# The running sum opens with the skip term, and a third buffer holds products of h and C

## What is computed

```python
dA = jnp.exp(dt[:, :, None] * A[None])
dBu = dt[:, :, None] * B[:, None, :] * u[:, :, None]

def step(hst, inp):
    dAt, dBut, Ct = inp
    hst = dAt * hst + dBut
    return (hst, hst @ Ct)
_, ys = lax.scan(step, jnp.zeros((D_INNER, D_STATE), h.dtype), (dA, dBu, C))
y = ys + u * D_skip
y = y * jax.nn.silu(z)
return y @ w_out
```

## Time and profile before

| | |
|---|---|
| median of 3 runs | 1579.28 us (1578.86 to 1580.91) |
| profiled execution | 1580.11 us |
| its span | 1578.3 us |
| TensorE busy | 1504.4 us, 95% |
| VectorE busy | 1360.7 us, 86% |
| GpSimd busy | 1134.1 us, 72% |
| ScalarE busy | 1025.7 us, 65% |
| TensorE's granted clock, mean | 0.986 |

### The profile page before, as it was taken

The page is one execution under the profiler, slowest core; times in us unless marked ns, Lnnn a source line. Parts: engine busy times, 40 slices in busy tenths (PEclk is TensorE's granted clock), DMA queues, the critical chain, the costliest instruction groups (busy, mean ns, idle before and its releaser), DMA issues. The chain is left out here.

```text
span 1578.3 us, 17939 instructions
## 1 busy us (share of the span) xinstructions
PE 1504.4 (95%) x4976; PEld 768.4 (49%) x4976; DVE 1360.7 (86%) x1617; ACT 1025.7 (65%) x2180; POOL 1134.1 (72%) x542
## 2 busy tenths in 40 slices
PE   7999999999999999999999999999997789999995
PEld 3444434444444444444444444444442235999994
DVE  7405999999999999999999999999999897667998
ACT  3254757666666767676767585757666755777774
POOL 0325989898989898989898898989898883000223
PEclk9999999999999999999999999999998899999998
DMA  9877767777777777676767777777752523000002
GB/s 364 336 244 275 256 230 243 246 252 243 257 244 259 244 238 263 233 260 240 244 238 259 243 249 254 248 252 248 252 190 73 181 74 118 16 0 1 0 0 107
DMA packets 65404, 322.46 MB, mean 204 GB/s; under 512 B 7036, under 2 KB 7088, under 8 KB 32437
## 3 DMA queue, kind: packets, MB, share of 16 engines
q1 hardware_dynamic: 54433, 302.21, 55.0%
q10 hardware_dynamic: 10900, 19.44, 4.2%
HBM read 309.27 MB, written 12.35 MB: 204 GB/s over the span
## 5 line engine op out<-in xcount | busy, mean ns | idle before, releaser
L655 PE MATMUL bank<-ring,xh 128*128 128x512 f32 x2048 | 956.7, 594 | 10.9 <-DVE xh L1296 8.1
L1428 DVE TENSOR_TENSOR_SCAN work<-bank,hstate,work 128x512 f32<-128x512 f32 x512 | 628.8, 1272 | 20.3 <-ACT bank L965 13.0
L655 PEld LDWEIGHTS bank<-ring,xh 128*128 128x128 f32 x2048 | 387.6, 190 | 462.6 <-issue 422.5
L1159 POOL TENSOR_TENSOR work<-work 128x1024 f32<-128x1024 f32 x210 | 495.8, 2361 | 85.5 <-DVE work L1369 77.1
L965 ACT ACTIVATE bank<-work,a_neg 128x512 f32<-128x512 f32 x512 | 344.6, 686 | 250.5 <-DVE work L1428 247.1
L1361 DVE TENSOR_TENSOR work<-work,bank 128x1024 f32<-128x1024 f32 x253 | 307.1, 1219 | 62.2 <-POOL work L1135 54.4
L1369 DVE TENSOR_TENSOR work<-work,bank 128x1024 f32<-128x1024 f32 x168 | 201.8, 1201 | 23.3 <-POOL work L1159 23.3
L541 PE MATMUL bank<-bc_parts,sel 96*128 96x512 bf16 x422 | 161.8, 384 | 23.5 <-DVE work L1361 22.6
L1245 POOL TENSOR_TENSOR work<-work 128x256 f32 x32 | 27.3, 854 | 213.2 <-ACT work L1032 213.2
L536 PE MATMUL bank<-work,w_sb 128*128 128x512 f32 (+2 forms) x352 | 175.3, 594 | 1.3 <-issue 0.8
L1104 POOL TENSOR_TENSOR work<-work 128x1024 f32<-128x1024 f32 x48 | 113.7, 2369 | 18.5 <-ACT work L839 18.4
(11 more groups left out here) (163 smaller groups left out, 1589.7 us busy)
## 6 DMA issues: line engine op xcount, KB each, us to landing
ring<-adj_t SPq DMA_DIRECT2D x256, 1024.0 KB, 5.4
xh<-c_scratch SPq DMA_DIRECT2D x34, 256.0 KB, 3.3
work<-c_scratch ACTq DMA_DIRECT2D x28, 256.0 KB, 5.9
c_two<-c_scratch ACTq DMA_DIRECT2D x28, 256.0 KB, 5.0
xh<-x_rows SPq DMA_DIRECT2D x16, 256.0 KB, 7.2
work<-x_t SPq DMA_DIRECT2D x16, 256.0 KB, 5.3
x_scratch<-work ACTq DMA_DIRECT2D x16, 256.0 KB, 3.6
work<-x_scratch SPq DMA_DIRECT2D x1, 4096.0 KB, 14.6
```

What stands on the lines that cost most here:

```text
L655: last = nc.tensor.matmul(mixed[:, :], xn[:, j, :], a, start=(j == 0), stop=(j == BLK - 1))
L1159: nc.gpsimd.tensor_tensor(out=acc, in0=hc[0] if n == 1 else acc, in1=hc[n % 2], op=ALU.add).then_inc(y_added, 1)
L1428: nc.vector.tensor_tensor_scan(hb[s % 2][:, h, :], da[h], (dbu_late[POOL_DBU.index(s)] if on_pool else dbu[s % 2])[:, h, :], hstate[:, HV ...
```

## The change

The accumulator `acc` takes over the role of `yv`. ScalarE writes the skip term of the chunk being scanned into `acc`, in slot 3 of the same k, once the gate of the chunk before has read `acc` (`y_ready`). GpSimd's `add(0)`, placed in slot 2 of its program ahead of `add(1)`, waits for the skip term and adds product 0; sixteen additions, all of the form acc + hc. The closing additions L1142 and L1348 go, and the gate reads `acc`. The buffer of `yv` becomes a third buffer for products: product n goes to `hc[(16c + n) % 3]` and waits for addition (or sum) n-3. The skip terms of the last two chunks stay in k = 17, and `dbu_late` uses `u[0]` instead of `acc`.

```diff
-        hc = [halves(carve(W2)) for _ in range(2)]
+        hc = [halves(carve(W2)) for _ in range(3)]
...
-        yv = halves(carve(W2))
...
+        def hc_of(c, n):
+            return hc[(DS * c + n) % 3]
...
-        dbu_late = [dt[0], dtu[0], acc]
+        dbu_late = [dt[0], dtu[0], u[0]]
...
                 def state_sum(n, c):
...
-                        pe.wait_ge(y_skip, k - 2)
+                        pe.wait_ge(hc_done, hc_count(NC - 3, DS - 1, False))
+                        wait(pe, y_skip, c - (NC - 2))
...
                 def skip(values):
                     for h in range(HV):
-                        last = nc.scalar.activation(yv[:, h, :], values[:, h, :], ACT.Copy, scale=V("d_skip", h))
+                        last = nc.scalar.activation(acc[:, h, :], values[:, h, :], ACT.Copy, scale=V("d_skip", h))
                     last.then_inc(skip_ready, 1)
 
                 def post_part(s):
-                    if s == 0 and k < NC + 2:
+                    if s == 0 and k == NC + 1:
+                        act.wait_ge(y_ready, NC - 2)
                         skip(u[q])
...
+                    if scan and not drains(k) and s == 3:
+                        wait(act, y_ready, cs)
+                        skip(u[par])
                     if scan and not drains(k) and s in C_LOAD:
                         load_c(C_LOAD[s])
...
-                        pool.wait_ge(y_added, (DS - 1) * (k - 2))
-                        pool.wait_ge(skip_ready, k - 2)
-                        nc.gpsimd.tensor_tensor(out=yv, in0=yv, in1=acc, op=ALU.add).then_inc(y_skip, 1)
...
-                    nc.gpsimd.tensor_tensor(out=by_step(yp), in0=by_token(yv), in1=by_token(sz[q]), op=ALU.mult).then_inc(y_ready, 1)
+                    nc.gpsimd.tensor_tensor(out=by_step(yp), in0=by_token(acc), in1=by_token(sz[q]), op=ALU.mult).then_inc(y_ready, 1)
 
                 def add(n):
 
                     wait_hc(pool, cs, n)
-                    if n == 1:
-                        wait_hc(pool, cs, 0)
-                    if n > 1:
-                        pool.wait_ge(y_added, (DS - 1) * cs + (n - 1))
-                    nc.gpsimd.tensor_tensor(out=acc, in0=hc[0] if n == 1 else acc, in1=hc[n % 2],
-                                            op=ALU.add).then_inc(y_added, 1)
+                    if n == 0:
+                        pool.wait_ge(skip_ready, cs + 1)
+                    else:
+                        pool.wait_ge(y_added, DS * cs + n)
+                    nc.gpsimd.tensor_tensor(out=acc, in0=acc, in1=hc_of(cs, n), op=ALU.add).then_inc(y_added, 1)
...
                     if drains(k):
-                        if n < 2:
-                            pool.wait_ge(y_added, (DS - 1) * (NC - 2))
-                        wait(pool, y_summed, DS * (cs - (NC - 2)) + (n - 1))
-                    elif n >= 2:
-                        pool.wait_ge(y_added, (DS - 1) * cs + max(n - 2, 1))
+                        if n < 3:
+                            pool.wait_ge(y_added, DS * (NC - 2))
+                        wait(pool, y_summed, DS * (cs - (NC - 2)) + (n - 2))
                     else:
-                        wait(pool, y_added, (DS - 1) * cs + (n - 1))
...
+                        wait(pool, y_added, DS * cs + n - 2)
...
                     elif scan and s >= 2:
+                        if s == 2:
+                            add(0)
                         add(s - 1)
...
                 def finish_y():
...
-                    if k == NC:
-                        dve.wait_ge(y_added, (DS - 1) * (NC - 2))
-                        nc.vector.tensor_tensor(out=yv, in0=yv, in1=acc, op=ALU.add).then_inc(y_skip, 1)
...
-                    wait(dve, y_added, (DS - 1) * cs + (max(n - 2, 1) if n >= 2 else n - 1))
-                    nc.vector.tensor_tensor(out=hc[n % 2], in0=hb[n % 2], in1=both(c_bank[n % 2]),
+                    wait(dve, y_added, DS * cs + n - 2)
+                    nc.vector.tensor_tensor(out=hc_of(cs, n), in0=hb[n % 2], in1=both(c_bank[n % 2]),
                                             op=ALU.mult).then_inc(hc_done, 1)
```

More of the change, by code:

```diff
@@ L582, in last_sums @@
                                 wait_hc(pe, NC - 1, n)
-                            last = nc.tensor.matmul(y_bank[h][:, :], ident, hc[n % 2][:, h, :], start=False, stop=(n == DS - 1))
+                            last = nc.tensor.matmul(y_bank[h][:, :], ident, hc_of(NC - 1, n)[:, h, :], start=False, stop=(n == DS - 1))
                         last.then_inc(y_half_done, 1)
@@ L590, in state_sum @@
                         pe.wait_ge(ident_ready, 2)
-                        pe.wait_ge(y_skip, k - 2)
+                        pe.wait_ge(hc_done, hc_count(NC - 3, DS - 1, False))
+                        wait(pe, y_skip, c - (NC - 2))
                     wait_hc(pe, c, n)
                     for h in range(HV):
-                        last = nc.tensor.matmul(y_bank[h][:, :], ident, hc[n % 2][:, h, :], start=(n == 0),
+                        last = nc.tensor.matmul(y_bank[h][:, :], ident, hc_of(c, n)[:, h, :], start=(n == 0),
                                                 stop=(n == DS - 1))
@@ L669, in step @@
                             for h in range(HV):
-                                nc.tensor.matmul(y_bank[h][:, :], ident, yv[:, h, :], start=False, stop=False)
+                                nc.tensor.matmul(y_bank[h][:, :], ident, acc[:, h, :], start=False, stop=False)
                         if k == NC:
@@ L1122, in pre_part @@
                         elif scan:
-                            pool.wait_ge(y_added, (DS - 1) * cs + 11)
+                            pool.wait_ge(y_added, DS * cs + 12)
                         else:
@@ L1165, in make_dbu @@
                     pool.wait_ge(scan_done, HV * DS * (NC - 1))
+                    if i == 2:
+                        pool.wait_ge(skip_ready, NC - 1)
                     nc.gpsimd.tensor_tensor(out=dbu_late[i], in0=dtu[par], in1=b_late[i].unsqueeze(1).broadcast_to([P, HV, CH]),
@@ L1180, in make_hc @@
                     if drains(k):
-                        if n < 2:
-                            pool.wait_ge(y_added, (DS - 1) * (NC - 2))
-                        wait(pool, y_summed, DS * (cs - (NC - 2)) + (n - 1))
-                    elif n >= 2:
-                        pool.wait_ge(y_added, (DS - 1) * cs + max(n - 2, 1))
-                    else:
-                        wait(pool, y_added, (DS - 1) * cs + (n - 1))
-                    nc.gpsimd.tensor_tensor(out=hc[n % 2], in0=hb[n % 2], in1=c.unsqueeze(1).broadcast_to([P, HV, CH]),
+                        if n < 3:
+                            pool.wait_ge(y_added, DS * (NC - 2))
+                        wait(pool, y_summed, DS * (cs - (NC - 2)) + (n - 2))
+                    else:
+                        wait(pool, y_added, DS * cs + n - 2)
+                    nc.gpsimd.tensor_tensor(out=hc_of(cs, n), in0=hb[n % 2], in1=c.unsqueeze(1).broadcast_to([P, HV, CH]),
                                             op=ALU.mult).then_inc(pool_hc_done, 1)
@@ L1317, in side_part @@
                     if drains(k):
-                        if post and k < NC + 2 and slot == (1 if k == NC else 2):
+                        if k == NC + 1 and slot == 2:
                             finish_y()
@@ L1345, in finish_y @@
                     dve.wait_ge(skip_ready, k - 2)
-                    if k == NC:
-                        dve.wait_ge(y_added, (DS - 1) * (NC - 2))
-                        nc.vector.tensor_tensor(out=yv, in0=yv, in1=acc, op=ALU.add).then_inc(y_skip, 1)
-                    else:
-                        dve.wait_ge(y_summed, DS)
-                        for h in range(HV):
-                            last = nc.vector.tensor_tensor(out=yv[:, h, :], in0=yv[:, h, :], in1=y_bank[h][:, :], op=ALU.add)
-                        last.then_inc(y_skip, 1)
+                    dve.wait_ge(y_summed, DS)
+                    for h in range(HV):
+                        last = nc.vector.tensor_tensor(out=acc[:, h, :], in0=acc[:, h, :], in1=y_bank[h][:, :], op=ALU.add)
+                    last.then_inc(y_skip, 1)
                 def both(ap):
@@ L1375, in make_last_hc @@
                     dve.wait_ge(scan_done, HV * DS * cs + HV * (n + 1))
-                    dve.wait_ge(y_summed, DS * (cs - (NC - 2)) + (n - 1))
+                    dve.wait_ge(y_summed, DS * (cs - (NC - 2)) + (n - 2))
                     for h in range(HV):
-                        nc.vector.tensor_tensor(out=hc[n % 2][:, h, :], in0=hb[n % 2][:, h, :], in1=c_bank[0][:, :],
+                        nc.vector.tensor_tensor(out=hc_of(cs, n)[:, h, :], in0=hb[n % 2][:, h, :], in1=c_bank[0][:, :],
                                                 op=ALU.mult).then_inc(last_hc, 1)
```

5 lines of the change are left out of this document (4 added, 1 removed).

## The result

The changed kernel took 1564.4 us (median of 4 runs, 1563.57 to 1567.1). The kernel before took 1580.1 us in four runs (1578.86 to 1581.81). The ratio is 0.9897, 95% interval 0.9885 to 0.9909: 1.0% faster, 15.7 us. The profiled execution took 1564.17 us with a span of 1562.3, against 1580.11 and 1578.3 before.

What follows compares the result with a forecast made beforehand. The prediction took TensorE's own 74.4 us a chunk as the bound. It summed 11.4 us (steady part), 2.8 (start of k=16) and 2.0 (k=17) to 16.2, giving 1563.1 us, range 1560.5 to 1573.

Steps and rivals of the forecast that it cites:

- What bounds: Periodic part: TensorE sets the pace, with 74.4 us of its own work in a chunk of 75.25 us.
- The wait at the turn: At each chunk's turn, VectorE's product 15 no longer waits for GpSimd's addition 13; VectorE gains 1.66 us a turn.
- The new wait w: Once a chunk VectorE's scan 5 waits for GpSimd's product 3, behind the skip term and additions 0 to 2: 1.5 us.
- Slack: VectorE's lead over TensorE at L1326: 0.4 us left; TensorE waits for nothing while the new scan wait is under 1.9.
- k=3: TensorE's wait at the turn to this chunk falls from 2.33 us by 1.55 to 0.78.
- k=4 to k=15: TensorE's waits of about 0.82 us at each of twelve turns go, 9.9 us in all; period 74.4 us.
- Start of k=16: VectorE loses the closing addition and waits around it; GpSimd caps the gain at 2.8 us, bounds 1.8 and 3.2.
- k=17: Chunk 15: GpSimd's waits for TensorE's sums go, so VectorE gains its 2.0 us of waits for products; bounds 0 and 2.7.
- A: Rival: the opening chain bounds; scan 5's wait is 1.9 to 2.9 us, VectorE sets the period, up to 1.0 x 12 lost; chance 0.22.
- B: Rival: nothing reaches the end; scan 5's wait is 2.9 us or a little above, time within 3 us of before; chance 0.08.
- C: Rival: slower; one more GpSimd instruction or equal delay in the opening chain, scan 5 waits 3.8 us, 1586 us; chance 0.06.
- D: Rival: the third buffer pays nothing in k=16 and 17 because TensorE's granted clock falls; 1568 us; chance 0.09.

Runs made afterwards that it cites:

- third_buffer_alone: The kernel before with three buffers for products of h and C; the sum's old opening and closing addition stay: 1565.65 us, ratio 0.9905.
- skip_twice: The changed kernel with ScalarE's skip term written twice, one after the other, 1.35 us more in the opening chain: 1584.16 us, ratio 1.0022.
- skip_slot2: The changed kernel with ScalarE's skip term one slot earlier, in slot 2: 1563.39 us, ratio 0.9885; run once more, 1563.41 us.
- product3_first: The changed kernel with GpSimd making product 3 before addition 2, skip term left in slot 3: 1564.51 us, ratio 0.9894.
- after_again: The changed kernel once more, unedited, as the measure beside other runs: 1566.52 us, ratio 0.9915.

## Why the prediction held, step by step

- *What bounds.* TensorE's own work of 74.4 us a chunk was right: 74.38 to 74.59 in every kernel where it doesn't wait for VectorE, and of that 0.1 to 0.2 are waits for the adjacency ring.
- *The wait at the turn.* Right. It is gone, and `third_buffer_alone` shows that the third buffer does it.
- *The new wait w.* The mechanism and place were right, the size was off: 2.03 for 1.5. The chain from the end of scan 2 (593.87) to the start of scan 5 (605.88) is 12.01 us where the sum said 11.7. GpSimd's part of it and ScalarE's are these rows:

```profile
593.90 0.69 ACT L970 ACTIVATE bank<-work,a_neg 128x512 f32<-128x512 f32 x1 [0.48 <-DVE work L1433]
594.53 0.19 ACT L952 ACTIVATE hstate<-work 128x2 f32<-128x2 f32 x1
594.63 1.32 ACT L902 ACTIVATE work<-work,v_sb 128x512 f32<-128x512 f32 x2
...
596.09 7.35 POOL L1167 TENSOR_TENSOR work<-work 128x1024 f32<-128x1024 f32 x3 [2.93 <-ACT work L902]
603.39 2.35 POOL L1195 TENSOR_TENSOR work<-work,c_two 128x1024 f32<-128x1024 f32 x1
```

  Exponential, small copy, skip and handoff took the 2.2 that they were given. The three additions took 7.30, not 6.93: each needs the one before it, and I had taken their pitch from two instructions that don't depend on each other (2.31), though the row of three dependent ones stood beside it (7.45 from 658.55 to 666.00). VectorE's own work meanwhile was 10.0, not 10.2. These two make the 0.5.
- *Slack.* The 0.4 forecast at L1326 came out as 0.45, with w larger than forecast by 0.5. VectorE is a little quicker elsewhere (its scans 1267 ns in the mean for 1272, its waits for the exponential 0.3 us a chunk for 0.5), which covers some 0.4 of it; the rest I haven't traced. The threshold of 1.9 was near the true one and stood in the wrong place: `skip_twice` shows that TensorE meets the delay at ScalarE's copies and silu, from w about 2.0. The cover of 1.3 us that the prediction gave to the move of the skip held at L835, and the wait for the skip, 3.0 us on GpSimd, is as forecast. What it did not trace are ScalarE's later instructions, L862 and L868, and GpSimd's convolution additions ahead of L868: it checked GpSimd's load against the chunk (68.9 and 3 in 74.4), not when each result comes.
- *k=3.* Forecast 1.55, measured 0.47 in k=3, with 0.13 lost in k=2. The wait at L544 fell as said (2.33 to 0.54, 0.78 forecast), but TensorE lost 0.82 of it again at L862 and L868, and another 0.5 is in no wait that the trace names. This is the term that failed, by 1.2 us, and the opening is the cause: `skip_slot2` and `third_buffer_alone`, whose k=3 takes 74.70 and 74.71, get all of the forecast 1.55 and more, and `product3_first`, with GpSimd's additions as late and no wait of scan 5, gets none of it back.
- *k=4 to k=15.* 9.9 forecast, 8.90 measured. No wait for the product is left, but TensorE's waits for the adjacency ring rose from 0.5 us in 2 to 2.0 in 7, and one chunk of 74.81 us has a w of 2.3. `skip_slot2` has ring waits too, 2.6 us in 9, and `third_buffer_alone`, without the opening, 1.5 in 6, so these don't come from the opening; that the faster pace brings them is likely and not shown. The prediction's "no DMA moves" was true and not enough.
- *Start of k=16.* 2.8 forecast, 2.1 measured: from the copy to scan 3 of chunk 14, 18.29 us before and 16.16 after. Product 0 took 2.33 us, as taken, not 3.33. But it starts 9.60 us after the copy where it was 8.36, since GpSimd now does addition 15 in the place where VectorE had closed the sum, so "it starts its products of chunk 14 where it did" was wrong by 1.2. And most of the gain isn't the closing addition's: `third_buffer_alone` keeps that addition and has 1.65 of the 2.1. Scan 2 waits for it:

```profile
1185.50 4.66 POOL L1195 TENSOR_TENSOR work<-work,xh 128x1024 f32<-128x1024 f32 x2
...
1187.98 2.46 DVE L1433 TENSOR_TENSOR_SCAN work<-bank,hstate,work 128x512 f32<-128x512 f32 x2 [0.97 <-POOL work L1195]
```

- *k=17.* 2.0 forecast, 3.2 measured. The scans of chunk 15, from the first product of dt*u and B to the end of the last scan, took 59.5 us and now 56.4. The forecast counted VectorE's 2.0 us of waits for GpSimd; most of the rest is, by its size, the 0.82 that L1352 waited for TensorE's sums. Neither wait is left in those scans, and GpSimd's 10.4 us of waits for sums are gone too.
- *The sum.* 14.9 us came from the change where 16.2 were forecast: -1.2 at k=3, -1.0 in the steady part, -0.7 at the start of k=16, +1.2 in chunk 15, and +0.3 in the stretches of the drain for which nothing was counted (0.1 between scan 3 and chunk 15's first product of dt*u and B, 0.26 after the last scan). That the span fell by 16.0, within 0.2 of the forecast, is luck in part: it owes 0.85 us to an early start of that one execution and 0.3 to its LSTM part, and within the 14.9 terms of either sign cancel. The medians are 15.7 us apart.
- *The rivals.* A had the right chain, and w = 2.03 even lies just inside its condition; its price there, 0.13 x 12 = 1.6 us, is near what the kernels without this wait gain. But VectorE doesn't set the period, and TensorE doesn't stop at the turn. B and C did not come. D did not either: the granted clock in the drain is 0.91 after and 0.90 before, and the waits of the earlier trace rows are gone, though the third buffer's own price there isn't settled. C's price was about right: it should decide from w = 3.3, and `skip_twice`, at 3.40, is 0.2% slower than before.

What stays open: the size of the third buffer's part in the drain, whether the opening is worth anything from end to end, the 0.4 us a chunk in `skip_twice`, and which of the two ways to ScalarE costs more there. Of what was run, `skip_slot2` has the lowest median, 1563.4 us in both series; beside the changed kernel in the same series it is 2.6 us lower, with no run of one within the range of the other.

## What to carry to other kernels

When a change moves a wait from one place to another, the price is not the wait but what it delays, and the slack read at one meeting point (0.45 us here) isn't the slack of the loop: follow each in-order queue that the late engine feeds, to its last consumer, and the late engine's own next results too. Price a chain of dependent instructions by a row of dependent ones. And separate what one edit buys from what another spends, here -15 us for the third buffer and +21 us for the opening without it.

## What the runs showed of the hardware

- Additions of 128x1024 in a row on GpSimd, each reading the accumulator that the last one wrote: three took 7.30 us up to the next instruction here and 7.45 in the earlier trace rows, against 3 x 2.31 = 6.93 between independent ones. A dependence costs 0.17 to 0.19 us a link (two links in the first, three in the second).
- A VectorE addition of 128x1024 takes 2.85 us when it meets GpSimd's additions with both inputs in SBUF, 1.19 with one in PSUM. In `third_buffer_alone` such an addition stood just behind GpSimd's: it took 1.23, and GpSimd's small select then took 1.18 for 0.29.
- In some executions of one and the same kernel TensorE's granted clock falls to its lower level (1.2 GHz) for a moment in the LSTM part, and in others not. In `after_again` it fell near 1422.8 us (the mean over 1420 to 1423 is 0.97). TensorE had been busy 19.6 of the 20 us up to 1420, then stood 1.95 us for VectorE and had resumed at 1422.55. The changed kernel's profiled execution has the same pause of 1.95 us, and its clock stayed at the upper level. The same 30 us of both (granted clock ahead of the last two columns):

```profile
1420.00:1450.00 30.00, 28.05 (x217) 27.00 (x216) 23.09 (x69) 19.38 (x76) 4.14 (x5) 0.94 0.00 1
```

```profile
1420.00:1450.00 30.00, 28.08 (x230) 27.10 (x231) 24.83 (x73) 20.55 (x81) 5.02 (x6) 1.00 0.00 1
```

  The LSTM part took 250.1 us in the first and 248.4 in the second, 1.7 us that no edit of these experiments touches, and about as much as the smallest differences between them.
